# Sampling with four corners: VectorE adds them in pairs, TensorE adds the two sums while it transposes

## The chip, the cores and the metric

The program runs on one core of one Trainium2 chip. The metric is the device time of one launch in microseconds (us); lower is better. Engines are named as in the profile: PE is TensorE, DVE is VectorE, ACT is ScalarE, POOL is GpSimd, SP is SyncE, which only issues transfers.

## What is computed

Four convolution-like layers follow each other on x (8 images, 64 channels, 56 x 56), each added to its input: a 7 x 7 neighbourhood average with learned weights, a 3 x 3 convolution, a deformable 3 x 3 convolution, and a state-space block. The change is in the third. Its reference, cut to what matters:

```
off  = conv(x, offset_w, offset_b)          # dy, dx of each of 9 taps
mask = 2 * sigmoid(conv(x, mod_w, mod_b))
py, px = base + tap + (dy, dx);  y0, x0 = floor(py), floor(px)
sampled = v00*(1-wy)*(1-wx) + v01*(1-wy)*wx + v10*wy*(1-wx) + v11*wy*wx
sampled = sampled * mask                    # [image, tap, y, x, channel]
out = einsum('bkhwc,ock->bohw', sampled, w2)
```

v00 to v11 are the values of x at the four grid points round (py, px), zero outside the image. All data are f32.

## The kernel before

The stage is `stage_flow`. Images go in four pairs; a pair's 2 x 3136 output points make NSEQ = 49 tiles of 128 points, 196 tiles in all (NTILE). A table in DRAM holds, for each grid point, its own channels and those of its three neighbours (4 x 64 values), so that one fetched row gives all four corners of one tap. Each tile T passes through these steps, each on its engine and in the order in which `program` lists them:

- GpSimd, `gather` (L863): nine indirect DMAs, one for each tap, each fetching 128 rows of 4 x 64 values into `quad[T % 4]`. It waits for the indices (`picked`) and for the product of tile T - 4 (`scaled`), which frees the buffer.
- ScalarE, `spread_coef` (L1255): copies the tile's 36 coefficients to PSUM (`cof`).
- VectorE, `scale` (L1014): `quad` times the coefficients, into `part[T % 2]`, 128 x (4 corners, 9 taps, 64 channels). `pick` (L1006) then copies the indices of tile T + 4, 128 x 9.
- VectorE, `corners` (L1022): a reduction over the four corners of `part` into `tap[T % 2]`, 128 x (9, 64).
- VectorE, `add` of tile T - 1 (L1032; L1037 for a pair's last tile): adds the projected result to `xres`.
- TensorE, `turn` (L1155): five transposes of `tap` (two taps each, the last one tap) into PSUM, after `reduced`, `copied` and `added` of the tiles concerned.
- ScalarE (L1267, L1268): copies them to SBUF. TensorE, `project` (L1164, L1165): ten matmuls with the layer's weights.

Between the tiles the same queues carry `prepare`, the preparation of the next image: pads of the normalised input on VectorE (L908) and ScalarE (L1195), the 3 x 3 convolution (L681, L683), the offsets (L1102, L1105, turned by the small products L1126), positions and coefficients on VectorE (`corner`, L938 to L950 with the comparison L941, and `weigh`, to L966 with L964), and `add_up`, which joins the next pair with the first layer's result (`join`, L878: 128 x 3136, both inputs in SBUF). Three joins meet gathers in time, the first comes before them.

Of the kernel before, what the change touches and what calls it, by code (L numbers as in the profile page):

```python
# [18 lines left out]
ALU = mybir.AluOpType  # L19
ACT = mybir.ActivationFunctionType  # L20
AX_X = mybir.AxisListType.X

P = 128
NB, CH, HH, WW = 8, 64, 56, 56
# [26 lines left out]
K2 = 9  # L51
TP = 2 * WW
NT = HH // 2
TS = 128
# [17 lines left out]
START = 1  # L72
# [615 lines left out]
def stage_flow(nc, k, xres, ident):  # L688
# [19 lines left out]
    with ExitStack() as ctx:  # L708
        s_ = Space(nc, ctx, "fl")
# [16 lines left out]
        idx = [s_.sb(f"idx{i}", [TS, K2], U32) for i in range(RQ)]  # L726
        quad = [s_.sb(f"quad{i}", [TS, K2, 4 * CH]) for i in range(RQ)]
        part = [s_.sb(f"part{i}", [TS, 4, K2, CH]) for i in range(2)]
        tap = [s_.sb(f"tap{i}", [TS, K2, CH]) for i in range(2)]
        smp2 = [s_.sb(f"smp2{i}", [P, NPR, TS]) for i in range(2)]  # L730
        smp1 = [s_.sb(f"smp1{i}", [CH, TS]) for i in range(2)]
        stats = s_.sb("stats", [P, NSTAT, 6])
# [7 lines left out]
        y = s_.sb("y", [P, PIX])  # L740
# [25 lines left out]
        spread, scaled, reduced, turned, copied, projected, added, stored = (  # L766
            s_.sem(x) for x in ("spread", "scaled", "reduced", "turned", "copied", "projected", "added", "stored"))
# [104 lines left out]
        def _(dve):  # L872
# [135 lines left out]
            def scale(T):  # L1008
                e, i = T % 2, T % RQ
                dve.wait_ge(gathered[i], (16 * K2) * (T // RQ + 1))  # L1010
                dve.wait_ge(reduced, START + T)
                dve.wait_ge(spread, START + T + 1)
                f = cof.rearrange("p (s k) -> p s k", s=4)
                dve.tensor_tensor(part[e][:], quad[i][:].rearrange("p k (s c) -> p s k c", s=4),  # L1014
                                  f.unsqueeze(3).to_broadcast([TS, 4, K2, CH]), ALU.mult).then_inc(scaled, 1)

            def corners(T):
                e = T % 2
                dve.wait_ge(scaled, START + T + 1)
                if T >= 2:  # L1020
                    dve.wait_ge(turned, START + T - 1)
                dve.tensor_reduce(tap[e][:], part[e][:].rearrange("p s k c -> p k c s"), AX_X, ALU.add)\  # L1022
                   .then_inc(reduced, 1)

            def add(T):
                q, s = T // NSEQ, T % NSEQ
# [13 lines left out]
            def tile(T):  # L1040
                if T == 0:
                    for i in range(RQ):
                        pick(i)
                scale(T)
                if T + RQ < NTILE:
                    pick(T + RQ)
                corners(T)
                if T:
                    add(T - 1)
# [12 lines left out]
        def _(pe):  # L1062
# [84 lines left out]
            def turn(T):  # L1147
                e = T % 2
                pe.wait_ge(reduced, START + T + 1)
                pe.wait_ge(copied, START + T)  # L1150
                pe.wait_ge(added, START + T)
                for r in range(NPR + 1):
                    taps_r = slice(2 * r, 2 * r + 2) if r < NPR else slice(K2 - 1, K2)
                    out = ps2[:, r, :] if r < NPR else ps1
                    ins = pe.transpose(out, tap[e][:, taps_r, :].rearrange("p k c -> p (k c)"), ident[:])  # L1155
                ins.then_inc(turned, 1)

            def project(T):
# [9 lines left out]
            def tile(T):  # L1168
                if T:
                    project(T - 1)  # L1170
                turn(T)
# [970 lines left out]
def layered_convs_kernel(nc, k):  # L2142
    with ExitStack() as ctx:
        ident = ctx.enter_context(nc.sbuf_tensor("ident", [P, P], F32))
        gn3 = ctx.enter_context(nc.sbuf_tensor("gn3", [P, 2, NB], F32))
        loaded = nc.alloc_semaphore("ident_loaded")
        k["flat"] = nc.dram_tensor("flat", [NB, FLAT + 2 * GUARD], F32).ap()
        k["y0"] = nc.dram_tensor("y0", [NB, CH, PIX], F32).ap()
        k["x3"] = nc.dram_tensor("x3", [NB, CH, PIX], F32).ap()
        k["c_rows"] = nc.dram_tensor("c_rows", [2, DS, QL], F32).ap()  # L2150
        k["tables"] = [nc.dram_tensor(f"table{q}", [2 * TAB, 4 * CH], F32).ap() for q in range(NPAIR)]
        with nc.Block() as block:
            @block.sync
            def _(sp):
                sp.dma_start(ident[:], k["c_ident"]).then_inc(loaded, 16)
                sp.wait_ge(loaded, 16)
        with nc.sbuf_tensor("x_all", [P, NPAIR, PIX], F32) as x_all, \
                nc.sbuf_tensor("mean_of_pair", [P, P], F32) as pair_mean, \
                nc.sbuf_tensor("diff_of_pair", [P, P], F32) as pair_diff:
            stage_load(nc, k, x_all, pair_mean, pair_diff)  # L2160
        stage_mix(nc, k, ident)
        with nc.sbuf_tensor("xres", [P, NPAIR, PIX], F32) as xres:
            stage_flow(nc, k, xres, ident)
            stage_norm3(nc, k, xres, gn3)
        stage_mamba(nc, k, ident, gn3)
# [135 lines left out]
```

## Time and profile before

| | us |
|---|---|
| median of 2 runs | 6248.24 |
| the two runs | 6243.54 and 6252.93 |
| span of the profiled execution (its own time isn't given separately) | 6244.6 |
| VectorE, GpSimd, TensorE busy in the span | 5012.8, 4904.1, 4411.3 |
| gathers of the sampling stage, first to last | 885.6 to 3119.9 |
| last add of the stage ends | 3134.4 |
| mean granted TensorE clock | 0.814 of full |

The span runs from the first to the last instruction. A row of the timeline gives start, duration, engine, line, operation, output and inputs with their shapes, and in brackets how long the engine stood idle before it and what released it. "issue" is time in which it waited for nothing that the profile shows. Durations that overlap slightly on one engine are those of neighbours in its pipeline.

### The profile page before, as it was taken

How to read it: one execution, taken by the hardware profiler on the slowest of the kernel's cores; microseconds unless marked ns; L12 is line 12 of the kernel's file. 1: busy time of each engine (PE TensorE's matmuls, PEld its weight loads, DVE VectorE, ACT ScalarE, POOL GpSimd, SP SyncE). 2: the span in 40 equal slices, each digit the busy share in tenths (PEclk: the TensorE clock that was granted, in tenths of full speed). 3: DMA queues.
4: the chain of work that ended last, by engine and by line, in shares of the span. 5: the costliest groups of instructions: out<-in, count | busy, mean ns of one | idle time of the engine just before them, and what ended most of it. 6: DMA issues, size and time to landing. Idle time of an engine off the chain costs nothing. (4 is left out here: it accounts for less than half of the span.)

```text
span 6244.6 us, 55481 instructions
## 1 busy us (share of the span) xinstructions
PE 4411.3 (71%) x14922; PEld 2398.8 (38%) x14922; DVE 5012.8 (80%) x3958; ACT 2533.4 (41%) x3949; POOL 4904.1 (79%) x3492
## 2 busy tenths in 40 slices
PE   3777656565555657463338888888888888888887
PEld 1566523332323233232214444444444444444443
DVE  5899736776766676666639999999999999999998
ACT  2222111111111111110026666666766766766664
POOL 1777627777777777777719999999999999999997
PEclk8887766656565656655569999999999999999999
DMA  6666623444434443443324544454454544444443
GB/s 165 133 135 136 139 79 104 123 114 145 123 104 133 127 123 105 135 116 114 104 79 149 165 157 154 161 162 148 160 163 147 169 151 156 160 153 162 155 152 120
DMA packets 379240, 855.17 MB, mean 137 GB/s; under 512 B 195672, under 2 KB 238576, under 8 KB 374580
## 3 DMA queue, kind: packets, MB, share of 16 engines
q1 hardware_dynamic: 294228, 619.96, 33.3%
q0 software_dynamic: 84672, 231.32, 12.4%
q8 instruction: 135, 2.21, 0.2%
q14 instruction: 205, 1.68, 0.1%
HBM read 768.83 MB, written 56.48 MB: 132 GB/s over the span
## 5 line engine op out<-in xcount | busy, mean ns | idle before, releaser
L863 POOL DMA_INDIRECT fl_quad<-table,fl_idx x1764 | 1697.3, 962 | 695.0 <-issue 536.7
L2097 POOL TENSOR_TENSOR ma_hc<-ma_h,ma_cc 128x784 f32<-128x784 f32 x1024 | 1882.2, 1848 | 235.8 <-DVE ma_h L1998 203.7
L1642 PE MATMUL ma_bank<-ma_hc,ident 128*128 128x392 f32 x4096 | 1528.0, 495 | 10.2 <-POOL ma_hc L2097 7.6
L1998 DVE TENSOR_TENSOR_SCAN ma_h<-ma_da,ma_state,ma_bank 128x784 f32<-128x784 f32 x768 | 1418.0, 1846 | 101.6 <-DVE ma_bank L1985 3.5
L1014 DVE TENSOR_TENSOR fl_part<-fl_quad,fl_bank 128x2304 f32<-128x2304 f32 x196 | 500.1, 2552 | 710.1 <-DMA fl_quad<-table,fl_idx 696.6
L1867 ACT ACTIVATE ma_da<-ma_dt,ma_a_neg 128x784 f32<-128x784 f32 x1024 | 948.2, 943 | 271.1 <-DVE ma_h L1998 176.6
L1985 DVE TENSOR_TENSOR ma_bank<-ma_dtu,ma_bank 128x784 f32<-128x784 f32 x1024 | 983.4, 960 | 80.5 <-PE ma_bank L1629 79.1
L1155 PE MATMUL fl_bank<-ident,fl_tap 128*128 128x128 f32 (+1 forms) x980 | 242.3, 409 | 937.4 <-DVE xres L1032 876.0
L1642 PEld LDWEIGHTS ma_bank<-ma_hc,ident 128*128 128x128 f32 x4096 | 705.3, 189 | 449.5 <-POOL ma_hc L2097 36.0
L1022 DVE TENSOR_REDUCE fl_tap<-fl_part 128x576 f32<-128x2304 f32 x196 | 796.5, 4064 | 0.1
L1629 PE MATMUL ma_bank<-ma_bc,ma_sel 96*128 96x512 bf16 (+1 forms) x2048 | 514.8, 333 | 376.2 <-DVE ma_h L1998 361.0
L1155 PEld LDWEIGHTS fl_bank<-ident,fl_tap 128*128 128x128 f32 (+1 forms) x980 | 162.7, 200 | 998.7 <-DVE fl_tap L1022 997.3
L1267 ACT COPY fl_smp<-fl_bank 128x512 f32<-128x512 f32 x196 | 114.9, 586 | 1054.4 <-PE fl_bank L1155 1054.4
L1998 DVE TENSOR_TENSOR_SCAN ma_h<-ma_da,ma_zcol,ma_bank 128x784 f32<-128x784 f32 x256 | 472.8, 1847 | 37.4 <-issue 4.4
L1629 PEld LDWEIGHTS ma_bank<-ma_bc,ma_sel 96*128 96x128 bf16 x2048 | 155.2, 98 | 894.0 <-DVE ma_h L1998 645.6
L565 POOL TENSOR_TENSOR mx_prodg<-mx_win,mx_wts 128x1176 f32<-128x1176 f32 x160 | 391.2, 2488 | 24.7 <-DMA mx_win<-flat 24.5
L1164 PE MATMUL fl_bank<-fl_smp,fl_wr 128*64 128x128 f32 (+1 forms) x1600 | 330.6, 376 | 69.2 <-ACT fl_smp L1268 67.2
L469 PE MATMUL mx_tps<-mx_xt,mx_band 128*128 128x128 f32 x1456 | 341.5, 410 | 34.3 <-ACT mx_xt L507 26.6
L1255 ACT COPY fl_bank<-fl_coef 128x36 f32<-128x36 f32 x196 | 37.5, 191 | 754.2 <-DVE fl_part L1014 748.0
L469 PEld LDWEIGHTS mx_tps<-mx_xt,mx_band 128*128 128x128 f32 x1456 | 309.3, 237 | 65.8 <-ACT mx_xt L507 36.8
L1164 PEld LDWEIGHTS fl_bank<-fl_smp,fl_wr 128*64 128x64 f32 x1600 | 262.9, 196 | 174.2 <-ACT fl_smp L1268 106.1
L666 POOL TENSOR_TENSOR mx_wts<-mx_wts,mx_mask 128x1176 f32<-128x1176 f32 x28 | 74.7, 2667 | 236.6 <-DVE mx_wts L615 195.7
(229 smaller groups left out, 6131.6 us busy)
## 6 DMA issues: line engine op xcount, KB each, us to landing
ma_cc<-c_rows SPq DMA_DIRECT2D x512, 784.0 KB, 4.3
mx_win<-flat SPq DMA_DIRECT2D x64, 878.0 KB, 10.3
fl_quad<-table,fl_idx POOLq DMA_INDIRECT x1764, 2.7
table<-fl_xt SPq DMA_DIRECT2D x64, 392.0 KB
mx_mask<-in_c_mask SPq DMA_DIRECT2D x56, 294.0 KB, 4.5
ma_xs<-ma_x SPq DMA_DIRECT2D x64, 196.8 KB, 5.6
ma_xs<-ma_x SPq DMA_DIRECT2D x64, 196.5 KB, 6.1
mx_xf<-flat SPq DMA_DIRECT2D x8, 816.0 KB, 15.8
```

Source lines behind the costliest of these rows:

```text
L469: ins = pe.matmul(ops[m], band[:, m, p, :], rhs, start=(p == 0), stop=(p == NPR - 1))
L863: gp.indirect_dma_start(quad[i][:, kk, :], None, table, bass.IndirectOffsetOnAxis(ap=idx[i][:, kk:kk + 1], axis=0))\
L1014: dve.tensor_tensor(part[e][:], quad[i][:].rearrange("p k (s c) -> p s k c", s=4), f.unsqueeze(3).to_broadcast([TS, 4, K2, CH]), ALU.mult) ...
L1022: dve.tensor_reduce(tap[e][:], part[e][:].rearrange("p s k c -> p k c s"), AX_X, ALU.add)\
L1155: ins = pe.transpose(out, tap[e][:, taps_r, :].rearrange("p k c -> p (k c)"), ident[:])
L1164: pe.matmul(out, wr2[:, r, :], smp2[e][:, r, cols], start=(r == 0), stop=False)
L1629: ins = pe.matmul(ps_bu[i % 2][:, at], sel[:, i, :], bc[g][:, at], start=True, stop=True)
L1642: ins = pe.matmul(ps_y[:, t, :], ident[:], hc[:, n % RH, at], start=False, stop=(n == DS - 1))
L1867: act.activation(da[:, i % RH, :], dt[g][:], ACT.Exp, scale=a_neg[:, i:i + 1]).then_inc(expd, 1)
L1985: dve.tensor_tensor(ps_bu[i % 2], dtu[g][:], ps_bu[i % 2], ALU.mult).then_inc(bud, 1)
L1998: dve.tensor_tensor_scan(h[:, i % RH, :], da[:, i % RH, :], ps_bu[i % 2], before, ALU.mult, ALU.add).then_inc(scand, 1)
L2097: gp.tensor_tensor(hc[:, i % RH, :], h[:, i % RH, :], cc[:, i % (NGRP * GRP), :], ALU.mult)\
```

## The change

The reduction over four corners is replaced by one addition of two halves of `part`, in place: corners 0 and 1 plus corners 2 and 3, 128 x 1152 elements each. TensorE then transposes both of the sums that remain and accumulates them in PSUM, ten operations a tile in place of five. The buffers `tap` are gone; `part` is now what the transposes read, so the wait for them moves from `corners` to `scale`, and `scale` no longer waits for `reduced`.

```diff
--- before.py
+++ after.py
@@ -726,7 +726,6 @@
         idx = [s_.sb(f"idx{i}", [TS, K2], U32) for i in range(RQ)]
         quad = [s_.sb(f"quad{i}", [TS, K2, 4 * CH]) for i in range(RQ)]
         part = [s_.sb(f"part{i}", [TS, 4, K2, CH]) for i in range(2)]
-        tap = [s_.sb(f"tap{i}", [TS, K2, CH]) for i in range(2)]
         smp2 = [s_.sb(f"smp2{i}", [P, NPR, TS]) for i in range(2)]
         smp1 = [s_.sb(f"smp1{i}", [CH, TS]) for i in range(2)]
         stats = s_.sb("stats", [P, NSTAT, 6])
@@ -1008,7 +1007,8 @@
             def scale(T):
                 e, i = T % 2, T % RQ
                 dve.wait_ge(gathered[i], (16 * K2) * (T // RQ + 1))
-                dve.wait_ge(reduced, START + T)
+                if T >= 2:
+                    dve.wait_ge(turned, START + T - 1)
                 dve.wait_ge(spread, START + T + 1)
                 f = cof.rearrange("p (s k) -> p s k", s=4)
                 dve.tensor_tensor(part[e][:], quad[i][:].rearrange("p k (s c) -> p s k c", s=4),
@@ -1017,10 +1017,7 @@
             def corners(T):
                 e = T % 2
                 dve.wait_ge(scaled, START + T + 1)
-                if T >= 2:
-                    dve.wait_ge(turned, START + T - 1)
-                dve.tensor_reduce(tap[e][:], part[e][:].rearrange("p s k c -> p k c s"), AX_X, ALU.add)\
-                   .then_inc(reduced, 1)
+                dve.tensor_tensor(part[e][:, 0:2], part[e][:, 0:2], part[e][:, 2:4], ALU.add).then_inc(reduced, 1)
 
             def add(T):
                 q, s = T // NSEQ, T % NSEQ
@@ -1152,7 +1149,9 @@
                 for r in range(NPR + 1):
                     taps_r = slice(2 * r, 2 * r + 2) if r < NPR else slice(K2 - 1, K2)
                     out = ps2[:, r, :] if r < NPR else ps1
-                    ins = pe.transpose(out, tap[e][:, taps_r, :].rearrange("p k c -> p (k c)"), ident[:])
+                    for y in range(2):
+                        ins = pe.matmul(out, part[e][:, y, taps_r, :].rearrange("p k c -> p (k c)"), ident[:],
+                                        start=(y == 0), stop=(y == 1), is_transpose=True)
                 ins.then_inc(turned, 1)
 
             def project(T):
```

## Rows read from the trace of the kernel before

**Rows 1.** Windows, stretch of the gathers: PE, PEld, DVE, ACT, POOL busy, clock, DMA.
```profile
885.60:3120.00 2234.40, 1224.36 (x4317) 705.25 (x4318) 1525.72 (x1127) 325.37 (x811) 1697.30 (x1764) 0.60 0.41 120
```

**Rows 2.** Waits, same stretch: us in total, times, longest.
```profile
DVE fl_part L1014 <- DMA fl_quad<-table,fl_idx: 692.2, 164, 28.8
POOL fl_quad L863 <- issue: 536.1, 1760, 0.3
```

**Rows 3.** Groups by line, GpSimd, same stretch: count, busy, mean ns, idle.
```profile
L863 POOL DMA_INDIRECT fl_quad<-table,fl_idx x1761 | 1694.3, 962 | 536.4 <-issue 536.1 <-DVE fl_part L1014 0.3
```

**Rows 4.** Two lines' instructions: duration ns least, median, greatest.
```profile
L878 DVE TENSOR_TENSOR xres<-xres,fl_y x4: 3403/3406/3426, 762.6 to 2242.5; 128x3136 f32<-128x3136 f32 x4
...
L941 DVE TENSOR_TENSOR fl_over<-fl_fl,fl_at x8: 627/628/629, 862.1 to 2781.1; 128x450 f32<-128x450 f32 x8
```

**Rows 5.** Timeline of one steady tile: start, duration, engine, line.
```profile
2006.91 2.55 DVE L1014 TENSOR_TENSOR fl_part<-fl_quad,fl_bank 128x2304 f32<-128x2304 f32 x1 [4.17 <-DMA fl_quad<-table,fl_idx]
...
2009.23 0.95 POOL L863 DMA_INDIRECT fl_quad<-table,fl_idx  x1 [0.30 <-issue]
...
2009.50 4.05 DVE L1022 TENSOR_REDUCE fl_tap<-fl_part 128x576 f32<-128x2304 f32 x1
2010.49 0.95 POOL L863 DMA_INDIRECT fl_quad<-table,fl_idx  x1 [0.30 <-issue]
```

**Rows 6.** Timeline round the join of the last pair.
```profile
2242.37 0.94 POOL L863 DMA_INDIRECT fl_quad<-table,fl_idx  x1 [0.30 <-issue]
2242.54 3.40 DVE L878 TENSOR_TENSOR xres<-xres,fl_y 128x3136 f32<-128x3136 f32 x1
...
2243.62 3.15 POOL L863 DMA_INDIRECT fl_quad<-table,fl_idx  x1 [0.30 <-issue]
```

**Rows 7.** Timeline round a comparison of the corner step.
```profile
1377.60 0.63 DVE L941 TENSOR_TENSOR fl_over<-fl_fl,fl_at 128x450 f32<-128x450 f32 x1
...
1377.65 1.39 POOL L863 DMA_INDIRECT fl_quad<-table,fl_idx  x1 [0.30 <-issue]
```

**Rows 8.** Timeline round a product of the coefficients.
```profile
1114.14 0.43 DVE L964 TENSOR_TENSOR fl_coef<-fl_lo 128x216 f32<-128x216 f32 x1
1114.15 0.95 POOL L863 DMA_INDIRECT fl_quad<-table,fl_idx  x1 [0.30 <-issue]
```

**Rows 9.** The gather line's instructions, from issue to landing.
```profile
DMA to landing us min/median/max: 2.6/2.7/10.0
```

**Rows 10.** Timeline, reduction and next gather, first tile and last but one.
```profile
901.15 4.05 DVE L1022 TENSOR_REDUCE fl_tap<-fl_part 128x576 f32<-128x2304 f32 x1
902.01 0.95 POOL L863 DMA_INDIRECT fl_quad<-table,fl_idx  x1 [0.30 <-issue]
...
3112.98 4.05 DVE L1022 TENSOR_REDUCE fl_tap<-fl_part 128x576 f32<-128x2304 f32 x1
3113.97 0.95 POOL L863 DMA_INDIRECT fl_quad<-table,fl_idx  x1 [0.30 <-issue]
```

**Rows 11.** Timeline, the same of a tile in which VectorE was late.
```profile
1145.01 4.05 DVE L1022 TENSOR_REDUCE fl_tap<-fl_part 128x576 f32<-128x2304 f32 x1
1145.30 0.94 POOL L863 DMA_INDIRECT fl_quad<-table,fl_idx  x1 [0.30 <-issue]
```

**Rows 12.** Timeline round a pad of the input.
```profile
2025.33 1.97 DVE L908 TENSOR_SCALAR fl_xp<-xres,fl_rstd,fl_nmr 64x3136 f32<-64x3136 f32 x1
...
2025.48 1.95 POOL L863 DMA_INDIRECT fl_quad<-table,fl_idx  x1 [0.30 <-issue]
```

**Rows 13.** Timeline behind the last gather.
```profile
3124.32 4.05 DVE L1022 TENSOR_REDUCE fl_tap<-fl_part 128x576 f32<-128x2304 f32 x1
...
3128.84 1.30 PE L1155 MATMUL fl_bank<-ident,fl_tap 128*128 128x128 f32 x5 [6.63 <-DVE xres L1032]
...
3133.97 0.46 DVE L1037 TENSOR_TENSOR xres<-fl_bank,xres 64x64 f32<-64x64 f32 x2 [5.28 <-PE fl_bank L1165]
```

**Rows 14.** Timeline of TensorE in a tile with the offsets' products.
```profile
1354.58 5.75 PE L1126 MATMUL fl_bank<-fl_fold,fl_om 96*128 96x27 f32 x26
```

## Prediction

> **What bounds the kernel now.** I read the engines' busy time in the stretch of the gathers first [rows 1]: of 2234.4 us GpSimd is busy 1697.3, VectorE 1525.7, TensorE 1224.4. That alone doesn't say who sets the pace, so the second view is the table of waits of the same stretch [rows 2]. VectorE's product (L1014) waited 692.2 us for gathered data, in 164 of 196 tiles; GpSimd's gather (L863) waited for nothing but its own "issue". Third, the gathers as a group [rows 3]: 1761 of them, 962 ns each, with 536.1 us of issue before them and 0.3 us behind VectorE. So 1694.3 + 536.4 = 2230.7 us, all of the 2230 us from 890 to 3120, is GpSimd issuing one gather after another: 0.95 busy + 0.30 issue = 1.25 us each, nine a tile, 11.25 us a tile. VectorE, on the same tile, needs about 2.6 (product) + 4.1 (sum of corners) + 0.3 (add) = 7 us and then waits. The time can only change through (a) what lies behind the last gather, or (b) what the gathers themselves cost.
>
> **The sum of the corners.** The reduction of 128x2304 to 128x576, 4.05 us, becomes one sum of two operands of 1152 elements each. Both are f32 in SBUF, as in the join of a pair (L878, 3136 elements, 3.406 us) and in the comparison L941 (450 elements, 0.628 us) [rows 4]. Their slope is (3.406 - 0.628)/2686 = 1.034 ns an element, so 1152 take 0.628 + 702 x 1.034 ns = 1.35 us. VectorE gets 4.05 - 1.35 = 2.70 us a tile, 529 us in all. This is worth nothing in the stretch: it lengthens waits that [rows 2] show already.
>
> **What it adds to the gathers.** The reduction has one input in SBUF and the product has one (its other is in PSUM). The new sum has two. In the trace of before, gathers run at 0.95 us beside products and reductions [rows 5], but not beside operations with two SBUF inputs. The join that starts at 2242.54 is the plainest [rows 6]: the gather at 2243.62 takes 3.15 us in place of 0.95. It ends at 2246.77, that is 0.83 us after the join's end (2245.94), so what it does after its blocked moment takes 0.83, and that moment lies 0.95 - 0.83 = 0.12 us after its start. The gather at 2242.37 had begun 0.17 us ahead of the same join and was not touched, although it ran beside it for 0.8 us: one short access early in the gather is all that is blocked. All three joins that meet gathers show this. The comparison L941 [rows 7] runs 1377.60 to 1378.23 across the gather of 1377.65: 1378.23 + 0.83 = 1379.06, and the gather ended at 1379.04 (1.39 us). L964, which began 0.01 us ahead of its gather, cost it nothing [rows 8]; 0.05 us ahead was enough in L941. So the rule of this trace: if the VectorE operation starts at least some 0.03 us before a gather starts, at s, and is still running 0.12 us after the gather's start p, the gather is late by (s + duration) - (p + 0.12), and everything behind it on GpSimd's queue with it, since the queue has no slack.
>
> With 1.35 us for the new sum and k = p - s for the next gather, the loss is 1.23 - k. The period is 1.25 us, so nearly every tile hits exactly one gather, and the loss is anywhere from 0 to 1.2 us by the phase. The phase isn't random: the product is released by the landing of the ninth gather (2.7 us after its issue in the median [rows 9]), the new sum starts where the reduction starts now, and a delay of the queue shifts both alike. In the first tile k = 902.01 - 901.15 = 0.86, the loss 0.37; in the last but one k = 3113.97 - 3112.98 = 0.99, the loss 0.24 [rows 10]; in the tile of rows 5 (2009.50 and 2010.49) it is 0.24 too. Done for all 196 reductions: the 165 tiles whose product waited for the gather have a mean of 0.33, together 54.8 us. The 31 others, where VectorE was late from other work, have other phases, such as k = 1145.30 - 1145.01 = 0.29 and a loss of 0.94 [rows 11]; their mean is 0.68, together 21.1. As they stand that is 75.9 us. With 2.70 us a tile given back, most of these 31 will find VectorE waiting too, and at 0.33 each they make 10.2: 65 us. I take 65, since lateness of a few us is what put those tiles out of phase, and keep 76 as the upper end of this point. Bounds of the rest: with 1.30 or 1.40 us for the sum, 66 or 86 in place of 76; with all sums 0.1 us earlier or later, 59 or 92; 0.3 us later, 118; if every sum began just ahead of a gather, 196 x 1.2 = 235; if the blocked access were none, 0.
>
> The pads (L908, also an operation that delays a gather: 1.95 us in place of 0.95 [rows 12]) and the joins stay as many; they start at another phase, which I put at 0 with +-5 us for 14 pads and three joins.
>
> The Trainium skill (SBUF — State Buffer, "Who interferes with whom") has both sides of this. It says that a VectorE instruction with two SBUF inputs contends with a GpSimd instruction that reads SBUF, and it also says that a tensor_tensor didn't stall DMAs, inferring that descriptor generation needs only the write interface. By the second statement the added cost would be nothing and the result that of the first rival; the join and L941 speak against it for this kind of gather.
>
> **The transposes.** TensorE does ten in place of five. Five take 1.30 us as a run [rows 13], so the other five add 1.30 at the lower clock and less at the higher, 255 us in all at most. In the stretch it lies under GpSimd's 11.25 us. The worst place is the tiles in which 26 small products of the offsets (5.75 us, L1126) stand between a tile's transposes and its projection [rows 14]; there the projection may come about as late as now (VectorE's 2.70 earlier, 1.30 + TensorE's wait later), and the add with it. What VectorE loses there it doesn't pass on: a gather of tile T needs the product of T - 4, some 30 us before, and 0.3 us is all that GpSimd ever waited for it [rows 3]. Cost 0; were that cover gone, 1.3 us a tile, 255.
>
> **The waits.** The product of T now waits for the transposes of T - 2, since they read its buffer. VectorE's add of T - 2, earlier on its own queue, already waited for the projection behind those transposes, so the wait ends before it is reached: 0. The wait taken from the reduction was as empty.
>
> **Behind the last gather** all is path: the last reduction starts at 3124.32, the transposes at 3128.84, the last add at 3133.97 [rows 13]. -2.70 for the sum, +1.30 for five transposes: -1.4 us.
>
> **Sum:** 65 - 1.4 = +64 us. On the profiled span of 6244.6 that is 6308; its own run time isn't given beside it, but the two runs (6243.5 and 6252.9) lie round that span, and on their median of 6248.2 it gives 6312 us, +1.0%. No stage behind this one changes.
>
> **Rivals.** (A) No stall, not slower: the early access of the gather isn't blocked by this sum. Then only the tail moves: 6248.2 - 1.4 = 6247. For it: a reader could take the 3.15 us as something particular to whole-pair joins; against it: L941, 450 elements, follows the same arithmetic to 0.02 us. Decides: whether the gather beside the sum shows 0.95. (B) Slower by over 2%: the same stall in the bad phase. If the sum starts 0.35 us or more nearer to the gather that follows it (later landing, a longer start of the product), the loss passes 125 us; at the far end it is 235, 6483; in the middle, 0.9 us a tile, 176 us, 6424. For it: the 31 late tiles show such phases; against it: 155 of the 165 tiles that wait for data lie between 0.2 and 0.5. (C) TensorE becomes the bound, +255 us, 6500: against it 1224 + 255 = 1479 busy us in 2234. (D) VectorE was the bound after all and 2.7 us a tile come back: 5719; the waits for landed data rule it out nearly wholly.
>
> **How the numbers follow.** The stall as counted 0.79; A 0.07; B 0.11; C, and D or anything else, 0.015 each. Within the counted case the ends are +38 (phase 0.1 earlier, a shorter sum, pads and joins in favour, the low base of the runs) and +107 (0.1 later, or a longer sum and late tiles as now, and the spread of the runs), 6286 to 6355, which leaves out A and most of B, 2 in 10. Two per cent, about what a measurement of this kernel can tell from no change, is 125 us: faster 0.02, within 0.86, slower 0.12.
>
> **What would show it.** In the profile of the changed kernel: the sum at 1.35 us in place of 4.05; one gather a tile at about 1.28 us (0.95 + 0.33), so a mean of L863 near 999 ns in place of 962, with 0.30 of issue unchanged; the stretch of the gathers some 65 us longer; VectorE's wait for gathered data up by about 500 us; ten transposes in 2.6 us; later stages alike. The prediction is wrong if all gathers stay at 0.95 (A), if the long one a tile takes 1.8 or more (B), or if GpSimd shows waits for L1014.

## The result and the profile after

The changed kernel takes 6324.35 us (median of 2 runs, 6324.01 to 6324.68) against 6248.24: ratio 1.0117, 95% interval 1.0088 to 1.0147. It is 76 us slower, on a forecast of 64. The profiled execution has a span of 6322.9 us, 78.3 more than that of before.

The stretch of the gathers by engine (windows view, same columns as [rows 1]):

```profile
889.89:3190.55 2300.66, 1350.62 (x5299) 874.72 (x5300) 1000.75 (x1127) 326.88 (x811) 1763.39 (x1764) 0.62 0.40 117
```

The stretch grew from 2234.4 to 2300.7 us, 66.3 more. VectorE is busy 1000.8 us in it where it was busy 1525.7: 525 us of its work are gone, and the stretch is longer. The two waits that answer to [rows 2]:

```profile
DVE fl_part L1014 <- DMA fl_quad<-table,fl_idx: 1260.1, 190, 27.5
...
POOL fl_quad L862 <- issue: 537.0, 1762, 0.3
```

VectorE now waits 1260.1 us for gathered data, where it waited 692.2 (this view runs a little past the stretch; up to the end of the last gather it is 1252.8). GpSimd still waits only for its own issue. The gathers as a group, answering to [rows 3] (this answer also holds the first wait, 156.2 us for the table, which lies ahead of the stretch):

```profile
L862 POOL DMA_INDIRECT fl_quad<-table,fl_idx x1764 | 1763.4, 1000 | 693.4 <-issue 537.0 <-DMA table<-fl_xt 156.2 <-DVE fl_part L1014 0.3
```

The issue time is as it was (537.0 us, 0.30 each), but the mean gather is 1000 ns in place of 962, busy time 1763.4 in place of 1697.3 us. So all 66 us are inside gathers. Which ones, the timeline shows; first the sum by its source line, then one tile, answering to [rows 5]:

```profile
L1020 DVE TENSOR_TENSOR fl_part<-fl_part x196: 1345/1357/1378, 905.3 to 3194.9; 128x1152 f32<-128x1152 f32 x196
```

```profile
2009.57 2.56 DVE L1014 TENSOR_TENSOR fl_part<-fl_quad,fl_bank 128x2304 f32<-128x2304 f32 x1 [6.12 <-DMA fl_quad<-table,fl_idx]
...
2011.76 0.95 POOL L862 DMA_INDIRECT fl_quad<-table,fl_idx  x1 [0.30 <-issue]
...
2012.16 1.36 DVE L1020 TENSOR_TENSOR fl_part<-fl_part 128x1152 f32<-128x1152 f32 x1
2013.02 1.32 POOL L862 DMA_INDIRECT fl_quad<-table,fl_idx  x1 [0.31 <-issue]
...
2014.64 0.95 POOL L862 DMA_INDIRECT fl_quad<-table,fl_idx  x1 [0.30 <-issue]
```

The product ends, the sum starts at 2012.16 and runs to 2013.52; the gather that starts in it at 2013.02 takes 1.32 us, the one ahead of it 0.95 and the one behind it 0.95 again. 2013.52 + 0.83 = 2014.35, and it ended at 2014.34. A tile in a worse phase, 0.31 us from the sum's start to the gather's, loses 0.91:

```profile
2001.77 1.36 DVE L1020 TENSOR_TENSOR fl_part<-fl_part 128x1152 f32<-128x1152 f32 x1
2002.08 1.86 POOL L862 DMA_INDIRECT fl_quad<-table,fl_idx  x1 [0.30 <-issue]
...
2004.25 0.95 POOL L862 DMA_INDIRECT fl_quad<-table,fl_idx  x1 [0.30 <-issue]
```

In four tiles the gather beside the sum takes 2.42 to 2.67 us, because a pad (L907) starts 0.03 to 0.12 us behind the sum's end:

```profile
905.30 1.36 DVE L1020 TENSOR_TENSOR fl_part<-fl_part 128x1152 f32<-128x1152 f32 x1
906.32 2.42 POOL L862 DMA_INDIRECT fl_quad<-table,fl_idx  x1 [0.30 <-issue]
906.70 1.92 DVE L907 TENSOR_SCALAR fl_xp<-xres,fl_rstd,fl_nmr 64x3136 f32<-64x3136 f32 x1
```

The sum ends at 906.66 and the pad at 908.62. The gather ends at 908.74, 0.12 us behind the pad and not 0.83: it got past the sum and was then held up a second time, near its own end. The trace of before has the same in [rows 12], where the pad ends at 2027.30 and the gather at 2027.43; so it is beside four of the 14 pads there, and beside the other ten the gather ends 0.82 us behind the pad.

Behind the last gather, answering to [rows 13]:

```profile
3189.60 0.95 POOL L862 DMA_INDIRECT fl_quad<-table,fl_idx  x1 [0.30 <-issue]
...
3194.94 1.36 DVE L1020 TENSOR_TENSOR fl_part<-fl_part 128x1152 f32<-128x1152 f32 x1
...
3196.77 2.37 PE L1153 MATMUL fl_bank<-ident,fl_part 128*128 128x128 f32 x10 [5.80 <-DVE xres L1029]
...
3202.97 0.46 DVE L1034 TENSOR_TENSOR xres<-fl_bank,xres 64x64 f32<-64x64 f32 x2 [6.34 <-PE fl_bank L1164]
```

From the end of the last gather (3190.55) to that of the last add (3203.43) there are 12.9 us, where there were 14.5. Ten transposes take 2.37 us, five took 1.30.

The span divides so (start of the first gather; first gather to end of last; from there to the last add; the rest): before 885.6, 2234.4, 14.5, 3110.2; after 889.9, 2300.7, 12.9, 3119.5. The differences are +4.3, +66.3, -1.6 and +9.3, together 78.3.

### The profile page after: what moved, and what is told of

It is laid out like the page before. It is cut to its first block and busy times, and to the rows that moved or that the text cites. A ratio compares the mean times of both kernels' runs of the same rounds, so it can differ in the third digit from the quotient of the medians.

```text
span 6322.9 us, 57247 instructions
## 1 busy us (share of the span) xinstructions
PE 4551.5 (72%) x15902; PEld 2573.0 (41%) x15902; DVE 4484.9 (71%) x3958; ACT 2535.3 (40%) x3949; POOL 4971.5 (79%) x3492
## 5 line engine op out<-in xcount | busy, mean ns | idle before, releaser
L862 POOL DMA_INDIRECT fl_quad<-table,fl_idx x1764 | 1763.4, 1000 | 693.4 <-issue 537.0
L1997 DVE TENSOR_TENSOR_SCAN ma_h<-ma_da,ma_state,ma_bank 128x784 f32<-128x784 f32 x768 | 1417.8, 1846 | 101.5 <-DVE ma_bank L1984 3.4
L1014 DVE TENSOR_TENSOR fl_part<-fl_quad,fl_bank 128x2304 f32<-128x2304 f32 x196 | 500.6, 2554 | 1282.4 <-DMA fl_quad<-table,fl_idx 1260.1
L1153 PE MATMUL fl_bank<-ident,fl_part 128*128 128x128 f32 (+1 forms) x1960 | 435.9, 403 | 884.6 <-DVE xres L1029 829.6
L1153 PEld LDWEIGHTS fl_bank<-ident,fl_part 128*128 128x128 f32 (+1 forms) x1960 | 350.5, 203 | 950.9 <-DVE fl_part L1020 937.6
L1997 DVE TENSOR_TENSOR_SCAN ma_h<-ma_da,ma_zcol,ma_bank 128x784 f32<-128x784 f32 x256 | 472.7, 1846 | 49.4 <-POOL ma_hc L2096 16.4
L469 PEld LDWEIGHTS mx_tps<-mx_xt,mx_band 128*128 128x128 f32 x1456 | 309.0, 236 | 66.3 <-ACT mx_xt L507 36.8
L1020 DVE TENSOR_TENSOR fl_part<-fl_part 128x1152 f32<-128x1152 f32 x196 | 266.1, 1358 | 0.1
```

The lines of the kernel that those rows point to most:

```text
L469: ins = pe.matmul(ops[m], band[:, m, p, :], rhs, start=(p == 0), stop=(p == NPR - 1))
L862: gp.indirect_dma_start(quad[i][:, kk, :], None, table, bass.IndirectOffsetOnAxis(ap=idx[i][:, kk:kk + 1], axis=0))\
L1153: ins = pe.matmul(out, part[e][:, y, taps_r, :].rearrange("p k c -> p (k c)"), ident[:], start=(y == 0), stop=(y == 1), is_transpose=True)
L1997: dve.tensor_tensor_scan(h[:, i % RH, :], da[:, i % RH, :], ps_bu[i % 2], before, ALU.mult, ALU.add).then_inc(scand, 1)
```

## The experiments

The theory: the sum has two inputs in SBUF; while it runs, a gather that starts behind it is held up, and the gather and all behind it are late by 1.23 - k us, k being the time from the sum's start to the gather's. Its rivals: the ten transposes or the wait that moved; any VectorE operation at this place, or its writing in place; a stall of fixed size. The stage behind the last add, which none of these edits touches, also took different times from program to program (3102 to 3120 us), so the stretch of the gathers tells more than the total. All are timed beside the kernel before, whose median was 6248 us in each comparison. In the texts on record "the changed kernel" is the one of the diff.

**The pair sum with one input.** A reduction over two elements, into a buffer of its own:

```diff
-dve.tensor_tensor(part[e][:, 0:2], part[e][:, 0:2], part[e][:, 2:4], ALU.add)
+dve.tensor_reduce(pairs[e][:], part[e][:].rearrange("p (a b) k c -> p b k c a", a=2), AX_X, ALU.add)
```

> The changed kernel with its pair sum as a reduction over two elements (one SBUF input) into a buffer of its own; the ten accumulating transposes stay. Theory (the sum's second SBUF input stops the gather's early access): every gather beside it at 0.95 us, the stretch of the gathers back to about 2234 us, in all some 70 us below the changed kernel, 6250 us. Rival (the ten transposes, or the product's new wait for them, cost the time): stays at about 6324 us, since both are unchanged.

Measured: 6258.6 us, ratio 1.0015 (1.0005 to 1.0024). The stretch of the gathers is 2234.6 us, as before, with all ten transposes and the moved wait in place. In the timeline the reduction runs 2.58 us across two gathers, longer than the sum, and both take 0.95:

```profile
2003.80 2.58 DVE L1021 TENSOR_REDUCE fl_pairs<-fl_part 128x1152 f32<-128x2304 f32 x1
2004.67 0.94 POOL L863 DMA_INDIRECT fl_quad<-table,fl_idx  x1 [0.30 <-issue]
2005.92 0.95 POOL L863 DMA_INDIRECT fl_quad<-table,fl_idx  x1 [0.30 <-issue]
```

The transposes and the wait cost the stretch nothing. The total is 9 us over the expected 6250 and 10 over the kernel before. The profiled span is 13.2 us over that of before, and this lies outside the stretch: 5.2 ahead of the first gather and 8.2 behind the last add, in stages that the change doesn't touch (taken up below).

**The same operation with one input in PSUM.** It keeps type, size, output in place and duration, and leaves corners 2 and 3 out of the result; ScalarE's next write of the coefficients, in the same bank, waits for the sum instead of the product.

```diff
-dve.tensor_tensor(part[e][:, 0:2], part[e][:, 0:2], part[e][:, 2:4], ALU.add)
+dve.tensor_tensor(part[e][:, 0:2], part[e][:, 0:2],
+                  nil.unsqueeze(2).unsqueeze(3).to_broadcast([TS, 2, K2, CH]), ALU.add)
```

> The changed kernel with the second operand of the sum replaced by a zero in PSUM, the same shape and engine time, written in place as before; it leaves corners 2 and 3 out of the result. Theory (two inputs in SBUF): the sum still takes about 1.36 us, gathers at 0.95 us, some 70 us below the changed kernel, 6250 us. Rival (the in-place write, or any tensor-tensor operation at this point, blocks the gather): one gather a tile still at about 1.3 us, 6324 us.

Measured: 6259.1 us in one run, stretch 2234.9 us. Timeline:

```profile
2002.66 1.35 DVE L1021 TENSOR_TENSOR fl_part<-fl_part,fl_bank 128x1152 f32<-128x1152 f32 x1
2003.53 0.95 POOL L863 DMA_INDIRECT fl_quad<-table,fl_idx  x1 [0.30 <-issue]
...
2004.78 0.95 POOL L863 DMA_INDIRECT fl_quad<-table,fl_idx  x1 [0.30 <-issue]
```

1.35 us of VectorE across a gather's start, and the gather takes 0.95. Neither a tensor-tensor operation at this place nor the write in place is enough to hold the gather up; with the second input in SBUF it is held up.

**The sum 0.54 us later.**

```diff
+for j in range(1):
+    dve.bn_stats(spare[:, j], base[:].rearrange("p t k -> p (t k)")[:, 0:STAT])
 dve.tensor_tensor(part[e][:, 0:2], part[e][:, 0:2], part[e][:, 2:4], ALU.add)
```

> The changed kernel with one operation with a single SBUF input (statistics of 448 elements, some 0.54 us) put before each sum, so that the sum starts 0.54 us later against the gathers. Theory (loss = 1.23 - k, k from the sum's start to the next gather's): k falls from about 0.9 to 0.36, the loss of a tile rises from 0.35 to 0.87 us, 193 tiles: about 100 us above the changed kernel, 6425 us. Rival (a stall of fixed size for each sum): as the changed kernel, 6324 us, the added 0.54 us being hidden in VectorE's wait.

Measured: 6409.8 us, ratio 1.0261 (1.0244 to 1.0278), stretch 2397.6 us, 97 more than the changed kernel's. The timeline of a tile (k = 0.33, the gather takes 1.83, 0.88 more) and the group of the gathers:

```profile
2018.30 0.63 DVE L1022 BATCH_NORM_STATS2 fl_spare<-fl_base 128x6 f32<-128x448 f32 x1
2018.84 1.34 DVE L1023 TENSOR_TENSOR fl_part<-fl_part 128x1152 f32<-128x1152 f32 x1
2019.17 1.83 POOL L863 DMA_INDIRECT fl_quad<-table,fl_idx  x1 [0.30 <-issue]
```

```profile
L863 POOL DMA_INDIRECT fl_quad<-table,fl_idx x1764 | 1860.5, 1055 | 693.5 <-issue 536.4 <-DMA table<-fl_xt 156.4 <-DVE fl_part L1015 0.6
```

The 195 gathers beside the sum are long by 168.4 us in all. Four of them were then held up by a pad for 1.3 us more each, 5.2 together; the sum's own share is 163, 0.84 a tile, where 0.87 was expected. The total is 85 us above the changed kernel's and not 100, as the part behind the last add is 13 shorter (3106.6 us).

**The sum 1.07 us later**, with two such operations (`range(2)`).

> The same with two such operations, 1.07 us. Theory: the sum's start now falls just behind the start of one gather, k = 0.9 - 1.07 + 1.25 = 1.08, so that the loss falls to about 0.15 us a tile: some 30 us below the changed kernel, 6290 us, although VectorE does 1.07 us more a tile; tiles whose k was above 1.1 pay over 1 us, some ten of them. Rival (a stall of fixed size): 6324 us; rival (a stall that grows with VectorE's work): above the run with one such operation.

Measured: 6281.5 us, ratio 1.0056 (1.0039 to 1.0072): 43 us less than the changed kernel, with over 200 us more VectorE work. It is still 33 above the kernel before. The stretch is 2269.5 us, 31 less than the changed kernel's; the other 12 lie outside it. The sum now starts 0.18 us behind a gather, which isn't touched, and has nearly ended when the next one makes its access (1.09 us, 0.14 more):

```profile
2019.05 1.15 DVE L1022 BATCH_NORM_STATS2 fl_spare<-fl_base 128x6 f32<-128x448 f32 x2
2019.94 0.95 POOL L863 DMA_INDIRECT fl_quad<-table,fl_idx  x1 [0.30 <-issue]
2020.12 1.34 DVE L1023 TENSOR_TENSOR fl_part<-fl_part 128x1152 f32<-128x1152 f32 x1
2021.19 1.09 POOL L863 DMA_INDIRECT fl_quad<-table,fl_idx  x1 [0.30 <-issue]
```

```profile
L863 POOL DMA_INDIRECT fl_quad<-table,fl_idx x1764 | 1732.4, 982 | 693.6 <-issue 536.4 <-DMA table<-fl_xt 156.5 <-DVE fl_idx L1006 0.6
```

191 gathers beside the sum lose 40.3 us, 35 of it, 0.18 each, without what pads add to four of them; 0.15 was expected. Of the tiles that were expected to pay over 1 us, ten in number, six did (k from 0.02 to 0.14 us). In 47 tiles the sum starts 0.02 to 0.13 us behind a gather, about when, by the prediction's arithmetic, that gather makes its access, and all 47 take 0.95 us: it matters which of the two starts first. A fixed stall and one that grows with VectorE's work both fall: the two runs lie 97 above and 31 below.

**The sum alone.** The kernel before, its reduction as two sums on VectorE, with five transposes:

```diff
-dve.tensor_reduce(tap[e][:], part[e][:].rearrange("p s k c -> p k c s"), AX_X, ALU.add)
+dve.tensor_tensor(part[e][:, 0:2], part[e][:, 0:2], part[e][:, 2:4], ALU.add).then_inc(halved, 1)
+dve.wait_ge(halved, START + T + 1)
+dve.tensor_tensor(tap[e][:], part[e][:, 0], part[e][:, 1], ALU.add)
```

> The kernel before with its reduction replaced by two sums on VectorE (1152 elements, then 576, with a wait between), five transposes as before. Theory: the first sum stalls a gather as in the changed kernel, 0.34 us a tile; between the sums the waiting gather gets its access, and the next gather starts after the second sum: some 66 us above the kernel before, 6314 us. If the second sum gets ahead of the waiting gather, 0.7 us a tile more, 6450 us. Rival (the transposes cause the time): 6248 us, since TensorE does what it did.

Measured: 6317.3 us, ratio 1.0111 (1.0095 to 1.0126), stretch 2301.9 us. Without one added transpose the loss is the changed kernel's. Timeline:

```profile
2011.31 1.36 DVE L1023 TENSOR_TENSOR fl_part<-fl_part 128x1152 f32<-128x1152 f32 x1
...
2012.25 1.24 POOL L864 DMA_INDIRECT fl_quad<-table,fl_idx  x1 [0.30 <-issue]
2012.70 0.76 DVE L1025 TENSOR_TENSOR fl_tap<-fl_part 128x576 f32<-128x576 f32 x1
```

The gather of 2012.25 ends at 2013.49, 0.82 after the first sum's end (2012.67), and the second sum starts at 2012.70: the second sum didn't hold up the waiting gather, although the two left only 0.03 us between them.

**The transposes alone.** The kernel before with each transpose done twice:

```diff
+for _ in range(2):
     ins = pe.transpose(out, tap[e][:, taps_r, :].rearrange("p k c -> p (k c)"), ident[:])
```

> The kernel before with each of its five transposes done twice (the second overwrites the first with the same values), ten a tile, reduction as before. Theory: hidden under the gathers, stretch 2234 us, total 6249 us with 1.3 us behind the last gather. Rival (ten transposes cost the state-space stage, which took 9 us more in the changed kernel's profile, by what they add to the program): 6258 us, with the 9 us behind the sampling stage.

Measured: 6250.3 us, ratio 1.0002 (0.9992 to 1.0011), stretch 2233.6 us, behind the last gather 15.5 us, 1.0 more. From the last add to the end 3106.7 us, not 3119: the number of transposes isn't what made the last stage longer.

**No sum on VectorE.** `corners` is left out, TensorE waits for the product and adds all four corners:

```diff
-pe.wait_ge(reduced, START + T + 1)
+pe.wait_ge(scaled, START + T + 1)
-    for y in range(2):
+    for y in range(4):
```

> The changed kernel without the sum on VectorE: TensorE adds all four corners by accumulating transposes, 20 a tile. Theory (only an operation with two SBUF inputs on VectorE costs the gathers anything): no long gather beside it, the stretch back at 2234 us; behind the last gather 1.36 us less on VectorE and 2.4 more on TensorE; some 65 us below the changed kernel, 6258 us. Rival (TensorE's work or its wait is part of the added time, or becomes the bound with 20): above 6270 us, and GpSimd waits for VectorE's product.

Measured: 6247.1 us, ratio 1.0000 (0.9990 to 1.0009), stretch 2233.6 us. TensorE's run of 20 transposes, and the gathers as a group:

```profile
2001.51 3.78 PE L1147 MATMUL fl_bank<-ident,fl_part 128*128 128x128 f32 x20 [4.64 <-DVE xres L1024]
```

```profile
L862 POOL DMA_INDIRECT fl_quad<-table,fl_idx x1762 | 1694.5, 962 | 536.7 <-issue 536.1 <-DVE fl_part L1014 0.6
```

Mean 962, the value of before, although TensorE has fifteen more transposes a tile than there. VectorE loses its whole 4.05 us a tile and the time stays: its work was never the bound. The total is 11 below the expected 6258: the stages outside the stretch took about what they took before (887.8 and 3107.5 us), and the part behind the last gather 12.5 us where 13.9 was expected.

**The changed kernel again.**

> The changed kernel as it is, timed again beside the kernel before. Theory (about 66 us in the stretch of the gathers, and some 10 us that its stages before and behind took more): if the 10 us are of the program, the difference stays near 76 us; if they are of the execution, it falls to about 65.

Measured: 6323.2 us, ratio 1.0117 (1.0102 to 1.0133), the stretch 2299.1 us, the part behind the last add 3119.5 us once more. So the 9 us come back with this program.

**The pads.** The pads [rows 12] hold gathers up in the kernel before too, by 18 us in all beside 14 of them. They have only one large input in SBUF (the other two are one value a row), so the condition found for the sum, two inputs in SBUF, doesn't cover them; what in them does it wasn't tried. These runs show what moving them is worth. First both halves of every pad on ScalarE, on the kernel before and on the one with 20 transposes:

```diff
 act.activation(rows[CH:P, 0:HH, 1:1 + WW], ...).then_inc(shifted, 1)
+act.activation(rows[0:CH, 1:1 + HH, 1:1 + WW], ...).then_inc(padded, 1)
```

> The kernel before with its 16 pads on VectorE (14 of them beside gathers, each delaying one by about 1.3 us, 18 us in all) given to ScalarE, which does its own half of each pad first. Theory (what VectorE holds is what gathers wait for, ScalarE holds nothing of it): some 17 us below the kernel before, 6231 us. Rival (the pads' delays are hidden, or ScalarE's 3 us more puts the preparation of the next image late): 6248 us or above.

Measured: 6236.5 us, ratio 0.9981 (0.9972 to 0.9990). The stretch is 2217.5 us, 16.8 less, but it starts at 895.8, where the kernel before started it at 885.6: the first image's two pads, 3.0 us each on ScalarE, stand on the path ahead of the first gather. The total missed the expected 6231 by 6. In the profile, taken of the slowest of its eleven runs, the part behind the last add is 4.3 us longer too.

> Both: four corners added by 20 accumulating transposes, and the pads on ScalarE. Theory: 17 us below the run with the 20 transposes alone. The stretch of the gathers near 2217 us. Rival: no gain over it.

Measured: 6238.6 us, ratio 0.9985 (0.9976 to 0.9994), stretch 2216.1 us: the stretch as expected, the total only 8.5 below the run with the transposes alone. It starts 5.5 us later (893.3), and the part behind the last add is 6.8 us longer (3114.3; where, is told below).

Then the first image's pads back on VectorE (`if 2 * q + h:` ahead of ScalarE's, the opposite ahead of VectorE's):

> The kernel before with the pads that meet gathers on ScalarE, but those of the first image, ahead of the first gather, left on VectorE. The run with all pads on ScalarE gained 17 us in the stretch of the gathers and began it some 7 us later. Theory: the 17 us without the late beginning, 6231 us, faster than both kernels. Rival (the late beginning was of the execution, not of the pads): 6237 us as that run.

Measured: 6227.8 us, ratio 0.9965 (0.9953 to 0.9977), start 888.2, stretch 2217.3 us, from the last add to the end 3107.8. It is 20 us faster than the kernel before and 95 faster than the changed one. The mean gather is below that of [rows 3]:

```profile
L863 POOL DMA_INDIRECT fl_quad<-table,fl_idx x1764 | 1680.3, 953 | 694.0 <-issue 536.4 <-DMA table<-fl_xt 156.9 <-DVE fl_idx L1008 0.6
```

## Why the prediction was right

**The bound.** It was GpSimd's queue, as [rows 2, 3] said: taking 525 us (the changed kernel) or all of the reduction (20 transposes) from VectorE gave nothing, and each us added to a gather came out in the span.

**The price of the sum.** Forecast 1.35 us from the join and the comparison, measured 1.357 in the median.

**The stall.** The rule was read from three joins and a few small operations, and it holds in all details that were tried. The loss of a tile was forecast at 0.33 us, 65 in all; 193 gathers beside the sum were long by 69.7, of which 5.2 come from the pads behind four of the sums: the sum's own share is 64.5, 0.33 a tile. With them the 14 pads cost 17.1 us (18.2 before) and the three joins 6.8 (6.6), close to the 0 that was put for their new phase; the remaining operations cost about 2.5 more. Together that is 66 us of busy time. For the sum, the condition (two inputs in SBUF) stands on the reduction and on the PSUM operand; the phase stands on the two delays, 0.84 for 0.87 and 0.18 for 0.15. Of the 31 tiles in which VectorE was late six are left, as was argued for taking 65 and not 76. Two sentences of it are too wide. A short access 0.12 us after the gather's start isn't "all that is blocked": it is so for the joins and the sum, but a pad can hold a gather up a second time, 0.12 us ahead of its end. And a sum that starts behind the gather doesn't hold it, even if it starts before those 0.12 us are over. Neither changes the forecast.

**The side of the transposes, the waits, the tail.** Ten transposes took 2.37 us where 2.6 was given; no cost in the stretch, by the repeated transposes and by the reduction over two; behind the last gather -1.6 us for -1.4.

**The rivals.** No stall (A): not in this kernel, but the PSUM operand shows that case. The bad phase (B): it needs the sum 0.35 us nearer to the next gather, and a delay of 0.54 us was worth 97 us on top, over 2% against before; the changed kernel wasn't there. TensorE as the bound (C): excluded with 20 transposes. VectorE as the bound (D): excluded by the same run.

**What was short.** The last line of that sum, "no stage behind this one changes": the part behind the last add took 9.3 us more, in both profiles of the changed kernel. With it the forecast would have been 73 of 76. The number of transposes is not the cause (doubled: 3106.7 us; 20 a tile: 3107.5), nor are gathers. The reduction over two and the PSUM operand have it as well (3118.4 and 3120.0), the delayed sums not (3106.6 and 3102.0). The traces show where it arises. VectorE's part of the state-space stage is a loop of seven turns (`eng.Fori` in `chunks`), and its first scan behind each of the six jumps back (L1998, in the changed kernel L1997) comes late:

```profile
4457.30 0.62 DVE L2005 SCALAR_TENSOR_TENSOR ma_xr<-ma_bank,ma_vec,ma_xr 128x392 f32<-128x392 f32 x1
4458.58 1.85 DVE L1998 TENSOR_TENSOR_SCAN ma_h<-ma_da,ma_zcol,ma_bank 128x784 f32<-128x784 f32 x1 [0.66 <-issue]
```

```profile
4529.13 0.61 DVE L2004 SCALAR_TENSOR_TENSOR ma_xr<-ma_bank,ma_vec,ma_xr 128x392 f32<-128x392 f32 x1
4532.34 1.84 DVE L1997 TENSOR_TENSOR_SCAN ma_h<-ma_da,ma_zcol,ma_bank 128x784 f32<-128x784 f32 x1 [2.59 <-POOL ma_hc L2096]
```

The first pair is of the kernel before, the second of the changed one. The six waits are 0.57 to 0.92 us in the kernel before and 2.59 to 3.03 in the changed one, 12.0 us more in all. They are 2.5 to 2.9 us in the reduction over two and the PSUM operand too, and at most 1.0 in both delayed sums, with the sum alone and with doubled or 20 transposes. What these scans wait for by the kernel had been done before (in the row shown, by 4529.22), and the GpSimd product that the row names is none of it; so the time seems to go in VectorE's own queue at the jump. Why the same jump takes 2 us longer in some programs stays open. It would take programs that differ only in where their instructions lie, which weren't tried. With 20 transposes and the pads on ScalarE the six waits are 1.7 to 1.9 us, 6.8 more in all than with the 20 transposes alone, and the part is 6.8 us longer. The waits aren't the only difference: the kernel before with all pads on ScalarE shows 3114.5 us without long waits, in the profile of its slowest run. The 4.3 us ahead of the first gather are of the same size as the differences among the other runs (884.6 to 891.9, pads on VectorE) and are put down to nothing.

The Trainium skill (SBUF — State Buffer, "Who interferes with whom") says that a VectorE instruction with two SBUF inputs contends with a GpSimd instruction that reads SBUF; the runs agree (0.33 us a tile with two, 0 with one of them in PSUM). Its other remark, that a tensor_tensor didn't stall DMAs, doesn't carry over to these gathers; the measurement decides.

## What to carry to other kernels

Here GpSimd issued indirect gathers back to back and its queue was the bound. In such a stretch judge an operation on VectorE by what it holds up as well as by how long it takes: a 4.05 us reduction with one SBUF input was free, a 1.36 us sum with two cost 0.33 us a tile. Look in the trace of before for any operation of the new kind beside the gathers; three joins and a comparison were enough to give rule and size. The loss goes by phase, so 1.07 us of idle work ahead of the sum took 31 us out of the changed kernel's stretch, though it stayed slower than the kernel before. Better is to give the operation to an engine that held no gather up in these runs (ScalarE for the pads, TensorE for the sum), but not where it stands ahead of the first gather.

## What the runs showed of the hardware

A gather of 128 rows by index costs 0.95 us on GpSimd and 0.30 of issue. A sum on VectorE with both inputs in SBUF holds it up if the sum starts first, by some 0.02 us or more (beside sums that started 0.02 us ahead of them, one gather took 2.14 us and another 0.94); the gather then ends 0.82 or 0.83 us behind the sum. A sum that starts behind the gather costs it nothing, whether by 0.02 or by 0.18 us. With one input in PSUM the sum cost it nothing. A pad (64x3136, one large input in SBUF) can hold a gather up at two places: some gathers end 0.82 us behind the pad, others 0.12, and in four tiles a sum held the gather at the first place and the pad behind it at the second. Between two sums 0.03 us apart the waiting gather got through.

What I had not expected is the last stage's time, which comes and goes with edits to another stage (3102 to 3120 us from the last add to the end over twelve programs). In the changed kernel the first VectorE instruction behind each jump back of that stage's loop came 2.6 to 3.0 us late, in the kernel before 0.6 to 0.9; why stays open.
